# Start of a fused random-feature and gated FFN kernel: transfers, sums and the weight-feature phase in another order

## The reference

```python
xn = (x - mean(x)) / sqrt(var(x) + 1e-5)
def rfs(z):   # ab = xis, AB = exp(xis)
    dots = einsum('...d,rd->...r', z, ab[:, None] * proj)
    corr = 0.5 * sum(z * z, -1)[..., None] * ab * ab
    return 1 / sqrt(1024) * AB * exp(dots - corr)
s = rfs(xn) @ rfs(input_weights).T
h = silu(xn @ w1.T * w1_s) * (xn @ w2.T * w2_s)      # 1024 -> 4096
h = gelu(h @ h1.T * h1_s)                            # 4096 -> 4096
h = gelu(h @ h2.T * h2_s)                            # 4096 -> 4096
y = x + s * silu(h @ w3.T * w3_s)                    # 4096 -> 1024
```

## Time and profile before

| | us |
|---|---|
| runs of the kernel | 3003.17 and 2743.23, median 2873.2 |
| profiled execution, its own time | 2743.11 |
| its span, slowest core (core 5) | 2741.5 |
| spans of the eight cores | 2736.6 to 2741.5 |
| PE busy | 2627.9 (96%) |
| first matmul of the FFN (L400) | 133.58 after the span's start |
| mean granted TensorE clock | 0.989 to 0.990 |

### The profile page before, as it was taken

How to read it: one execution, slowest core, us unless ns; L and a number is a source line. 1 busy time by engine, 2 the same in 40 slices (tenths; PEclk the granted TensorE clock), 3 DMA queues, 4 the chain that set the end, 5 groups by cost and what they waited for, 6 DMA issues and landing times.

```text
span 2741.5 us, 28225 instructions; the slowest of 8 cores (2736.6 to 2741.5 us)
## 1 busy us (share of the span) xinstructions
PE 2627.9 (96%) x12054; PEld 1182.7 (43%) x12054; DVE 251.3 (9%) x382; ACT 354.4 (13%) x493; POOL 205.4 (7%) x391
## 2 busy tenths in 40 slices
PE   1799999999999999999999999999999999999997
PEld 0344444444444444444444444444444444444443
DVE  2123000000022300000002310000002210000001
ACT  0212010101111101010111200101011210101010
POOL 1010000000010000000001000000000000000000
PEclk9899999999999999999999999999999999999999
DMA  9078999999789999999978999999968999999995
GB/s 157 14 116 137 156 152 152 153 152 152 113 159 166 145 152 153 152 154 153 152 125 145 153 156 153 152 153 152 153 112 167 146 158 151 156 153 152 153 153 101
DMA packets 67115, 396.25 MB, mean 145 GB/s; under 512 B 7328, under 2 KB 11696, under 8 KB 21936
## 3 DMA queue, kind: packets, MB, share of 16 engines
q0 software_dynamic: 57408, 377.51, 88.4%
q1 hardware_dynamic: 9584, 16.92, 2.4%
HBM read 763.51 MB, written 8.39 MB: 282 GB/s over the span
## 4 chain that ended last, share of the span: by engine, by line
PE 96%; DMA 1%; DVE 1%; ACT 1%; issue 0%; POOL 0%; DVEq 0%; ACTq 0%
PE pb L483 65%; PE pb L527 8%; PE pb L400 8%; PE pb L423 8%; PE pb L356 2%; PE pb L373 2%; DMA xt_sweep<-xT 1%; PE pb L332 1%; ACT t L540 0%; PE pb L242 0%; PE pb L244 0%; ACT h_sb L494 0%; DVE xn_fm L279 0%; DVE xn_fm L280 0%; ACT L540 0%
## 5 line engine op out<-in xcount | busy, mean ns | idle before, releaser
L483 PE MATMUL pb<-h_sb,wring 128*128 128x512 bf16 x4096 | 884.7, 379 | 0.0
L483 PE MATMUL pb<-g_sb,wring 128*128 128x512 bf16 x4096 | 884.7, 379 | 0.0
L483 PEld LDWEIGHTS pb<-h_sb,wring 128*128 128x128 bf16 x4096 | 400.5, 98 | 484.8 <-issue 2.3
L483 PEld LDWEIGHTS pb<-g_sb,wring 128*128 128x128 bf16 x4096 | 400.8, 98 | 483.3
L527 PE MATMUL pb<-h_sb,wring 128*128 128x512 bf16 x1024 | 233.0, 391 | 18.8 <-ACT t L540 18.8
L423 PE MATMUL pb<-xn_fm,wring 128*128 128x512 bf16 x1024 | 231.5, 379 | 0.2 <-issue 0.2
L400 PE MATMUL pb<-xn_fm,wring 128*128 128x512 bf16 x1024 | 231.5, 379 | 0.0
L547 DVE TENSOR_TENSOR s_sb<-t,s_sb 128x512 f32<-128x512 bf16 x32 | 22.2, 692 | 2014.4 <-ACT t L540 2011.6
L494 ACT ACTIVATE h_sb<-pb,h2s_c 128x512 bf16<-128x512 f32 x128 | 87.9, 687 | 795.8 <-PE pb L483 786.9
L494 ACT ACTIVATE g_sb<-pb,h1s_c 128x512 bf16<-128x512 f32 x128 | 87.9, 687 | 692.9 <-PE pb L483 683.7
L527 PEld LDWEIGHTS pb<-h_sb,wring 128*128 128x128 bf16 x1024 | 102.4, 100 | 148.8 <-issue 34.9
(11 more groups left out here) (71 smaller groups left out, 392.1 us busy)
## 6 DMA issues: line engine op xcount, KB each, us to landing
wring<-h1p POOLq DMA_DIRECT2D x128, 1024.0 KB, 10.5
wring<-h2p POOLq DMA_DIRECT2D x128, 1024.0 KB, 10.4
wring<-w1p POOLq DMA_DIRECT2D x32, 1024.0 KB, 14.1
wring<-w2p POOLq DMA_DIRECT2D x32, 1024.0 KB, 11.0
wring<-w3p POOLq DMA_DIRECT2D x32, 1024.0 KB, 10.2
xt_r<-xT SPq DMA_DIRECT2D x32, 256.0 KB, 7.0
y<-s_sb SPq DMA_DIRECT2D x32, 256.0 KB, 6.4
xt_sweep<-xT POOLq DMA_DIRECT2D x32, 128.0 KB, 13.0
```

The costliest lines, as they stand in the source:

```text
L483: ii = t.matmul(p[quad[og]][:, :], wring[:, slot, k8, og * 128:(og + 1) * 128], src_sb[:, kk * 8 + k8, :], start=(kk == 0 and k8 == 0), st ...
```

## The change

Two things are put in another order.

1. On POOL the transfer of `projT` is issued after the row `xis` and no longer first. It still stands ahead of the five ring tiles.
2. `emit_wphase` is split. Its first part, `emit_so` (the 16 sums of the squared input weights and the two copies), now comes before the squares and the statistics of x. Its second part, `emit_wmms` (the 144 matmuls and their evictions), now comes after `ln2_bcast_affine`. Both parts use banks 2 and 3 where they used 4 and 5.

```diff
-        cast_sem["projT"] = Ctr(nc, stack, "cs_projT", g)
-        g.dma_start(projT_sb[:, 0:8, :], projT.rearrange("(j p) r -> p j r", p=128))\
-            .then_inc(cast_sem["projT"].sem, 16)
-        cast_sem["projT"].n = 16
         cast_sem["iwT"] = Ctr(nc, stack, "cs_iwT", g)
...
         g.dma_start(projT_sb[0:1, 8, :], xis[None, :]).then_inc(cast_sem["xisrow"].sem, 16)
         cast_sem["xisrow"].n = 16
+        cast_sem["projT"] = Ctr(nc, stack, "cs_projT", g)
+        g.dma_start(projT_sb[:, 0:8, :], projT.rearrange("(j p) r -> p j r", p=128))\
+            .then_inc(cast_sem["projT"].sem, 16)
+        cast_sem["projT"].n = 16
...
-        ln2_squares(0, 0)
-
         wstate = {}
 
-        def emit_wphase():
+        def emit_so():
             need(t, cV, sq_done)
             need(t, cast_sem["iwT"], 16)
-            guard_bank(4)
-            guard_bank(5)
+            guard_bank(2)
+            guard_bank(3)
...
-            bank_guard[4] = (cS, e1)
-            bank_guard[5] = (cS, e2)
+            bank_guard[2] = (cS, e1)
+            bank_guard[3] = (cS, e2)
+            wstate["e2"] = e2
+
+        def emit_wmms():
             need(t, cast_sem["projT"], 16)
             need(t, cast_sem["xisrow"], 16)
-            need(t, cS, e2)
+            need(t, cS, wstate["e2"])
             need(t, cV, cols_ready)
             ev = 0
             for rc in range(8):
                 for oh in range(2):
-                    bk = 4 + oh
+                    bk = 2 + oh
...
+        emit_so()
+        ln2_squares(0, 0)
         ln2_stats(0)
-        emit_wphase()
         xn_ready_sweep = ln2_bcast_affine(0, 0)
+        emit_wmms()
```

More of the change, by code:

```diff
@@ L298, in build_nc @@
                 iw_c[j], iw_c[j]))
-        ln2_squares(0, 0)
         wstate = {}
-        def emit_wphase():
+        def emit_so():
             need(t, cV, sq_done)
             need(t, cast_sem["iwT"], 16)
-            guard_bank(4)
-            guard_bank(5)
+            guard_bank(2)
+            guard_bank(3)
             for j in range(8):
                 sqv = h_sb[:, 2 * j:2 * j + 2, :].rearrange("p a b -> p (a b)")
-                t.matmul(p[4][0:1, :], ones_nh[:, 0:1], sqv[:, 0:512],
+                t.matmul(p[2][0:1, :], ones_nh[:, 0:1], sqv[:, 0:512],
                          start=(j == 0), stop=(j == 7))
-                ii = t.matmul(p[5][0:1, :], ones_nh[:, 0:1], sqv[:, 512:1024],
+                ii = t.matmul(p[3][0:1, :], ones_nh[:, 0:1], sqv[:, 512:1024],
                               start=(j == 0), stop=(j == 7))
@@ L317, in emit_wphase @@
             need(sc, cT, so_done)
-            e1 = S(lambda: sc.copy(iw_c[8][0:1, 0:512], p[4][0:1, :]))
-            e2 = S(lambda: sc.copy(iw_c[8][0:1, 512:1024], p[5][0:1, :]))
-            bank_guard[4] = (cS, e1)
-            bank_guard[5] = (cS, e2)
+            e1 = S(lambda: sc.copy(iw_c[8][0:1, 0:512], p[2][0:1, :]))
+            e2 = S(lambda: sc.copy(iw_c[8][0:1, 512:1024], p[3][0:1, :]))
+            bank_guard[2] = (cS, e1)
+            bank_guard[3] = (cS, e2)
+            wstate["e2"] = e2
+        def emit_wmms():
             need(t, cast_sem["projT"], 16)
             need(t, cast_sem["xisrow"], 16)
-            need(t, cS, e2)
+            need(t, cS, wstate["e2"])
             need(t, cV, cols_ready)
```

## The result

The changed kernel took 2712.01 us (median of 11 runs), against 2744.23 us for the kernel before (median of 10); 2711.7 had been predicted.
The medians are then 2711.4 and 2743.5 us: 32.1 us or 1.2% faster, ratio 0.9883. The ratio of the means is 0.9864 (95% interval 0.9819 to 0.9908), as the mean of before also counts a run of 2779.84 us, 35 us or more above the others. Either way the gain is clear of no change and within 2%, as forecast. The profiled execution took 2710.07 us, with spans of 2704.8 to 2708.5 us.

The account below looks back on a forecast made before the run. PE was taken as the bound, so the question was how early it reaches the FFN: 51.3 + 2.0 + 31.1 + 15.5 + 2.3 = 102.2, against 133.58. Thus 2743.1 - 31.4 = 2711.7 us, range 2706 to 2726.

Parts of the forecast that it names:

- The landings: Start transfers on POOL's queue: input weights land at 26.8 us, x at 33.4, projT at about 47.4.
- the half: The transfers' part of the gain: 14 of the 15.0 us by which the statistics are done sooner.
- The sums: PE's 32 one-column sums ahead of the row work: begin at 33.3 us, take 9.05, end at 42.4.
- R4: Rival: the one-column sums all run at half clock, 4.6 us less gain, 2716; chance within the forecast's 0.80.
- The row work: VectorE's statistics rows, first copy to end of last row: 8.6 us, from 42.6 to 51.2.
- the lower bound: Low end, 2706: 2.1 us for sums at full clock, 1.3 for the table load, about 2 for earlier landing.
- The clock's price: PE at half clock after its idle time before the spreading: 2.3 us, paid once where before it was paid twice.
- The first FFN matmul: End of the start phase on PE: 102.2 us against 133.58, 31.4 us earlier.
- Behind it: Everything after the FFN's first matmul: later ring transfers move with PE, the remainder costed at nothing.
- R1: Rival: queue place brings nothing, input weights and x land at 40.8 and 47.4; gain 17.5 us, 2725.6; chance 0.08.
- R2: Rival: projT becomes the new wait, landing with the last ring tile at 77.2; 2735.6; chance 0.09, wholly or in part.
- R3: Rival: in the large layers the ring-tile stream can't keep up, slower than before, up to about 2799; chance 0.02.

Follow-up runs that it names:

- e1: Kernel before with only the transfer of projT moved behind the row xis, code order and banks unchanged: 2730.55 us against 2742.66.
- e8: Changed kernel with the sums of the input weights and ScalarE's two copies put back behind the statistics: one time, 2744.33 us, not compared.
- e2: Changed kernel with projT issued first in the queue again, so only the code order and banks differ from before: 2724.67 us against 2742.66.
- e4: Changed kernel with projT issued behind two or all five ring tiles: 2717.93 us behind two, 2735.73 us behind five.
- e6: Changed kernel with x behind projT in the queue and weight features cut in three around statistics and spreading, over four banks: 2705.55 us, once.
- e5: Changed kernel with SP's first four residual loads (1 MB) held back until the FFN's first layer of sweep 0 is done: 2707.3 us.
- e7: Changed kernel with the edits of both e5 and e6: 2698.45 us against 2744.2 for the kernel before, ratio 0.9834.

## Why the prediction was right, point by point

- *The landings.* Input weights at 26.8 predicted, squares at 26.79 measured; projT at 47.4 predicted, 48.0 measured. x was put at 33.4 and came at 35.1, as it needed 8.3 us behind the input weights and not 6.6. This did no harm: PE's sums of the input weights ran meanwhile, and PE waited 0.19 us for the squares of x. The prediction's doubt, that landings might stray by a few us from their place in the queue, thus came to 1.7 us for x and 0.6 us for projT. e1 shows the half by itself.
- *The sums.* 33.3 predicted, 33.31 measured; the statistics reached VectorE at 43.18 and not 42.6. Only the first eleven of the 32 sums stood 0.42 us apart (33.31 to 37.95), the others 0.216, so R4 did not come about.
- *The row work.* 8.6 us had been taken; it was 43.18 to 50.57, 7.4 us. The difference is the table load of 1.28 us that went ahead of the copies: in e8, where it is back ahead of the Ln, the row work takes 8.6 us again (44.80 to 53.41). The prediction had left it in place and put its absence in the lower bound. The Trainium skill (ScalarE: Activation LUTs, "Table sets: the hidden batching unit") says that cheap functions such as copy are in every set. The trace agrees for the one set it shows: the set loaded at 39.29 ahead of the copy served the Ln and Exp of the statistics too, with no further load before them.
- *The clock's price.* This term was undersized: 2.3 us taken, 3.7 measured. It is the term of the sum that was furthest off. The spreading took 3.7 us (50.72 to 54.40) and not 2.0, and the weight features 33.07 us (to 87.47) and not 31.1. The windows of the changed kernel (us, busy PE, PEld, DVE, ACT, POOL, granted clock, DMA share, GB/s), answering to the earlier trace rows:

```profile
43.00:50.70 7.70, 0.01 (x1) 0.01 (x1) 4.91 (x8) 1.44 (x2) 0.00 (x0) 0.84 1.05 177
50.70:54.40 3.70, 3.68 (x5) 1.16 (x5) 0.00 (x0) 0.00 (x0) 0.00 (x0) 0.50 1.03 168
54.40:58.30 3.90, 3.90 (x11) 1.42 (x11) 3.24 (x5) 0.00 (x0) 0.00 (x0) 0.50 1.03 166
58.30:87.40 29.10, 29.10 (x136) 13.19 (x135) 8.17 (x13) 11.67 (x15) 0.00 (x0) 1.00 0.56 97
```

  The clock fell to 1.2 GHz while PE was idle, stayed there through the whole spreading and another 3.9 us of weight features, 7.6 us in all. The prediction had taken the price from matmuls of 128 partitions that follow a pause at once (1.8 and 2.7 us).
- *The first FFN matmul.* 102.2 predicted, 103.01 measured. The misses nearly cancel: the statistics 0.6 us later, the row work 1.2 us shorter, the clock 1.4 us dearer.
- *Behind it.* The rest was costed at nothing. From the first FFN matmul to the end of the span it was 2607.9 us on the slowest core before and 2605.5 now, 2.4 us less. One difference stands out and brings nothing in the end. In the statistics of sweep 1 the clock fell before (16 sums 4.9 us from the first start to the last, on all eight cores) and does not now on six of eight (3.2 us). The windows of before, then of now at the same place in the program:

```profile
229.00:239.00 10.00, 8.00 (x30) 2.74 (x29) 2.49 (x4) 0.00 (x0) 0.53 (x1) 0.83 1.01 160
```

```profile
198.00:208.00 10.00, 8.01 (x37) 3.13 (x36) 3.54 (x6) 0.09 (x1) 0.53 (x1) 1.00 0.92 135
```

  The 1.7 us gained there are lost again in the token features of sweep 1, in which the clock is now low for a while (0.87 and 0.95 in the windows 673.0 to 682.0 and 682.0 to 693.0, where at the same place before it was 1.00). Before and now:

```profile
712.05 15.70 PE L356 MATMUL pb<-xn_fm,projT_sb 128*128 128x512 bf16 x72 [2.54 <-ACT h_sb L494]
```

```profile
679.79 17.31 PE L359 MATMUL pb<-xn_fm,projT_sb 128*128 128x512 bf16 x72 [2.55 <-ACT h_sb L497]
```

  Behind them both kernels stand 594 us after the first FFN matmul. Of the 2.4 us, 1.4 lie in the very last store: from its issue to the end of the span it was 6.2 us before (2741.5 - 2735.26) and 4.8 now (2708.5 - 2703.71).

```profile
2735.26 2.72 SPq L559 DMA_DIRECT2D y<-s_sb  x4
```

```profile
2703.71 2.72 SPq L562 DMA_DIRECT2D y<-s_sb  x4
```

  On cores 0 to 3 this store took 4.8 to 4.9 us before as well, so the change of order does not explain it. The other 1 us was not traced. The forecast of 2711.7 thus met 2712.01 partly by luck: the FFN began 0.8 us too late, and the rest, put at nothing, came out shorter.
- *The rivals.* R1 (2725.6) is what e2 ran to (2724.67), and e1 shows that its premise is false. R2 (2735.6) is what e4 behind five tiles ran to (2735.73); the changed kernel keeps 6.4 us of slack. In both the FFN began later than priced (1.3 and 2.0 us), and a shorter rest made up for it (2605.7 and 2606.1 us on their slowest cores, against 2607.9). R3 did not show: L486's matmuls take 884.7 us as before, with no idle time.

## What to carry to other kernels

At a kernel's start, queue the transfers in the order of their first use, and compute for each the time at which it is needed: one that has slack is free to be late, and each us beyond it cost about one here. The order of first use is itself a choice: with the weight features begun early, as in e6, x could stand last. When work is reordered so that two engines run beside each other, give the two pieces different PSUM banks; with shared ones the old wait returns in another place. Loads that are read much later belong out of the start altogether, on whatever queue they run.

## What the runs showed that was not expected

- How long PE is idle does not tell what the clock costs behind it. Pauses of 5.17, 13.40 and 24.13 us (the last in e4 behind five tiles, weight features 33.73 us and not 31.1) cost 1.8, 2.7 and 2.6 us on the slowest cores; the pause of 7.71 us cost 3.7. What runs first behind it differs: there it is the spreading, float32 matmuls of one partition. In e8 the same spreading stands behind a pause of 5.48 us and the price is 3.5 us (spreading 3.7 and not 2.0, weight features 32.9 and not 31.1). That speaks for what runs first and against the length of the pause, but no run puts other matmuls in its place.
- The granted clock of a window is not the whole story. It reads 1.00 from 33.3 to 37.9, where the sums of the changed kernel stand 0.42 us apart, twice the full-clock distance. The distance from start to start is the safer measure.
- Taking 1 MB of SP's loads out of the start was worth 4.1 us in e5 and 7.1 us between e6 and e7, with x in another place of the queue. The second is near the 6.2 us that 1 MB costs in e4; the first is smaller because x came only 4.1 us sooner.
